# The first unit's q projected from unsplit fp32 weights, the k and v weights split first, and small loads moved back

## What is computed

```python
x = x + layernorm(attn(layernorm(x), w_qkv, b_qkv, w_out, b_out))
x = x + layernorm(ffn(layernorm(x), gate_w, up_w, down_w, scales))
# attn: 16 heads of 32, chunks of 128 tokens
qkv = x @ w_qkv.T + b_qkv                        # 3 x 512 outputs
out = (q * decay_q) @ S + ((q @ k.T) * dmask) @ v    # per chunk
S   = lam_c * S + (k * decay_k).T @ v
# ffn: silu(x @ gate * gs) * (x @ up * us) @ down * ds
```

## Time and profile before

| | |
|---|---|
| time of the runs | 993.68 us median of 3 (993.26 to 994.0) |
| profiled execution: its time | 993.01 us |
| profiled execution: its span | 991.2 us |
| PE busy | 957.7 us (97%) |
| DVE busy | 694.2 us (70%) |
| POOL busy | 686.9 us (69%) |
| ACT busy | 507.8 us (51%) |

### The profile page before, as it was taken

How to read it: one execution, slowest core, us unless ns; L and a number is a source line. 1 busy time by engine, 2 the same in 40 slices (tenths; PEclk the granted TensorE clock), 3 DMA queues, 4 the chain that set the end, 5 groups by cost and what they waited for, 6 DMA issues and landing times.

```text
span 991.2 us, 21995 instructions
## 1 busy us (share of the span) xinstructions
PE 957.7 (97%) x8498; PEld 709.6 (72%) x8498; DVE 694.2 (70%) x1355; ACT 507.8 (51%) x985; POOL 686.9 (69%) x837
## 2 busy tenths in 40 slices
PE   7999999999887999999999999999999999999996
PEld 6777778776665776777677677767767776776764
DVE  6999998875878766767676676767667676765422
ACT  3656665565555544646354464635446463544522
POOL 2689999887666765859476585947658594765733
PEclk9999999999998999999999999999999999999999
DMA  9899899999598784837558383866838486612200
GB/s 314 214 274 271 257 276 294 283 255 289 150 203 202 151 163 92 192 72 175 120 131 165 87 192 79 167 124 132 182 66 191 85 166 125 128 55 43 39 28 22
DMA packets 297641, 159.88 MB, mean 161 GB/s; under 512 B 141632, under 2 KB 272832, under 8 KB 297408
## 3 DMA queue, kind: packets, MB, share of 16 engines
q1 hardware_dynamic: 296672, 157.86, 67.5%
q10 hardware_dynamic: 864, 0.61, 0.2%
HBM read 82.93 MB, written 41.94 MB: 126 GB/s over the span
## 4 chain that ended last, share of the span: by engine, by line
PE 58%; DVE 17%; issue 10%; POOL 9%; ACT 4%; DMA 1%; POOLq 0%; SPq 0%; DVEq 0%; ACTq 0%
PE bank L845 17%; PE bank L827 12%; PE bank L720 9%; PE bank L735 8%; PE att L720 7%; POOL att_pool L996 4%; DVE stats L1249 3%; DVE p L1290 3%; DVE state_hl L1320 3%; DVE w_pool L1380 2%; ACT w_pool L562 2%; POOL rstd L937 2%; POOL w_pool L1010 2%; PE att L804 2%; DVE state L1309 1%
## 5 line engine op out<-in xcount | busy, mean ns | idle before, releaser
L827 PE MATMUL bank<-f_pool,gate_q 128*128 128x256 f16 x1536 | 183.9, 273 | 4.5 <-ACT w_pool L562 4.1
L827 PE MATMUL bank<-f_pool,up_q 128*128 128x256 f16 x1536 | 183.5, 273 | 1.4
L845 PE MATMUL bank<-down_q,w_pool 128*128 128x512 f16 x768 | 168.3, 379 | 0.0
L827 PEld LDWEIGHTS bank<-f_pool,gate_q 128*128 128x128 f16 x1536 | 146.9, 98 | 26.8 <-ACT w_pool L562 6.7
L827 PEld LDWEIGHTS bank<-f_pool,up_q 128*128 128x128 f16 x1536 | 149.3, 98 | 22.1 <-DVE w_pool L1380 5.0
L996 POOL TENSOR_TENSOR att_pool<-p,att_pool 128x512 f16<-128x512 f32 x128 | 145.7, 1160 | 26.3 <-ACT att_pool L516 26.3
L1380 DVE SCALAR_TENSOR_TENSOR w_pool<-bank,us_t,w_pool 128x256 f32<-128x256 f32 x192 | 84.1, 480 | 112.5 <-PE bank L827 54.1
L934 POOL TENSOR_TENSOR rstd<-mv,eps_t 128x1 f32<-128x1 f32 (+1 forms) x112 | 30.0, 268 | 182.6 <-DVE mv L1252 182.6
L845 PEld LDWEIGHTS bank<-down_q,w_pool 128*128 128x128 f16 x768 | 74.0, 98 | 87.0
L1010 POOL TENSOR_TENSOR w_pool<-w_pool 128x512 f16<-128x512 f32 x96 | 111.3, 1163 | 28.8 <-ACT w_pool L568 28.8
L516 ACT CAST att_pool<-p 128x512 f16<-128x512 f32 x128 | 75.5, 615 | 56.4 <-DVE p L1290 56.4
(11 more groups left out here) (143 smaller groups left out, 1824.9 us busy)
## 6 DMA issues: line engine op xcount, KB each, us to landing
xr<-in_x SPq DMA_DIRECT2D x32, 512.0 KB, 4.6
dram_qk<-qk_hl SPq DMA_DIRECT2D x64, 256.0 KB, 3.4
att_pool<-dram_qk SPq DMA_DIRECT2D x64, 256.0 KB, 5.6
f_pool<-dram_qk SPq DMA_DIRECT2D x64, 256.0 KB, 5.6
dram_kd<-kd_hl SPq DMA_DIRECT2D x32, 256.0 KB, 3.0
dram_v<-vv SPq DMA_DIRECT2D x32, 256.0 KB, 3.5
qn_pool<-dram_qk SPq DMA_DIRECT2D x32, 256.0 KB, 6.3
out_x<-w_pool SPq DMA_DIRECT2D x32, 256.0 KB, 2.1
```

Of the source, the lines that this page charges most:

```text
L827: ins = nc.tensor.matmul(b[:, j * TOK:(j + 1) * TOK], w[:, k, o * P:(o + 1) * P], x1_hl[:, v % 2, part, k], start=(k == 0 and part == 0), ...
L845: ins = nc.tensor.matmul((b_gate, b_up)[t][:, :], h_hl[:, part, k, t * P:(t + 1) * P], down_q[:, k], start=(k == 0 and part == 0), stop=(k ...
```

## The change

For unit 0 the four q outputs are no longer three 16-bit products each but one fp32 product: PE transposes the normalised x of unit 0 itself (`turn_first`), ACT copies it out of the bank into `x_first`, and `project_first` multiplies it with the weights as they were loaded, unscaled. ACT applies the scale while it reads the result (`scale=small[:, 11:12]`). The 136 constant products become 58. The weight split goes k, v, q instead of q, k, v, and ACT normalises x of unit 1 between k and v. The biases of v and the three scales are loaded by ACT later; the bias maximum is read from a table of 12 columns. x of unit 0 is loaded and normalised tile by tile. The product that spreads the maximum of the output weights moves from unit 2 to unit 3.

```diff
+            def turn_first(t):
+                pe.wait_ge(nrm_d[LN_X], t + 1)
+                for k in range(KT):
+                    ins = nc.tensor.transpose(b_s[t][:, k * P:(k + 1) * P], x_src(0)[:, t, k * P:(k + 1) * P], eye)
+                ins.then_inc(x_first_mm, 1)
+
+            def project_first(o):
+                for k in range(KT):
+                    ins = nc.tensor.matmul(qk_bank(0, o // 2)[:, o % 2 * TOK:(o % 2 + 1) * TOK],
+                                           w_stage[:, k, o * P:(o + 1) * P], x_first[:, k], start=(k == 0),
+                                           stop=(k == KT - 1))
+                if o % 2:
+                    ins.then_inc(qk_mm, 1)
...
-                if i == 0:
+                if i == 0 or n == 0 and i == 2:
                     pe.wait_ge(*x_landed(n))
+                if n == 1 and i == 0:
+                    pe.wait_ge(w_lo_d, 6)
...
-                        if n == 0 and j == 0 and (i == 0 and k % 2 == 0 or i == 2 and k == 0):
-                            pe.wait_ge(w_lo_d, i + k // 2 + 1 if i == 0 else 4)
+                        if n == 0 and i == 2 and j == 0 and k % 2 == 0:
+                            pe.wait_ge(w_lo_d, k // 2 + 1)
...
-                    pe.wait_ge(w_lo_d, 6)
+                    pe.wait_ge(w_lo_d, 4)
...
-                if k == 2:
+                if k == 3:
                     spread_wout_max()
-                project_qk(k, 0)
-                project_qk(k, 1)
+                if k:
+                    project_qk(k, 0)
+                    project_qk(k, 1)
...
-            for n in range(100):
-                nc.tensor.matmul(b_up[:, 0:2 * P], warm[:, 0:P], warm, start=True, stop=True)
+            constant_products(40)
+            pe.wait_ge(eye_in, 16)
+            turn_first(0)
+            constant_products(6)
+            turn_first(1)
+            constant_products(12)
+            pe.wait_ge(x_first_d, 2)
+            for k in range(KT):
+                pe.wait_ge(w_in[k], 16)
+            project_first(0)
             spread_w_max()
-            for n in range(36):
-                nc.tensor.matmul(b_up[:, 0:2 * P], warm[:, 0:P], warm, start=True, stop=True)
+            project_first(1)
+            project_first(2)
+            project_first(3)
...
-            act.dma_start(bv[:, :], b_v).then_inc(bias_in, 16)
+            act.wait_ge(eps_d, 3)
+            nc.scalar.activation(small[:, 63:64], eps_t[:, 0, 0:1], ACT.Silu)
+            x_normalise_tile(0, 0)
+            x_hi_tile(0, 0)
+            x_normalise_tile(0, 1)
+            x_first_tile(0)
+            x_hi_tile(0, 1)
+            x_first_tile(1)
+            act.dma_start(bv[:, :], b_v).then_inc(bv_in, 16)
...
-            x_normalise(0)
-            x_hi(0)
             act.wait_ge(w_scale_d, 1)
-            for part in range(3):
+            for part in (1, 2, 0):
                 for half in range(2):
                     w_hi(third(wqkv_hi, part, half), third(w_stage, part, half))
-            x_normalise(1)
-            x_hi(1)
+                if part == 1:
+                    x_normalise(1)
+                    x_hi(1)
...
+                dve.wait_ge(bias_in, 16)
+                link(nc.vector.tensor_reduce(col(7), bqk[:, :], AX.X, ALU.max, apply_absolute_value=True))
+                nc.vector.tensor_scalar(col(4), col(7), 1.0 / 256.0, None, ALU.mult)
...
-                    if k == 1:
-                        dve.wait_ge(bias_in, 16 * N_BIAS)
-                        nc.vector.tensor_reduce(col(7), bqk[:, :], AX.X, ALU.max, apply_absolute_value=True)
-                        link(nc.vector.tensor_reduce(col(8), bv[:, :], AX.X, ALU.max, apply_absolute_value=True))
-                        link(nc.vector.tensor_tensor(col(7), col(7), col(8), ALU.max))
-                        nc.vector.tensor_scalar(col(4), col(7), 1.0 / 256.0, None, ALU.mult)
...
-                link(nc.vector.tensor_scalar(bv[:, :], bv[:, :], col(11), None, ALU.mult))
-                for part in range(3):
-                    for half in range(2):
-                        w_lo(2 * part + half, third(wqkv_lo, part, half), third(wqkv_hi, part, half),
-                             third(w_stage, part, half))
...
-            moments_x(0)
+            for t, landed in enumerate((x_first_in, x_in[0])):
+                dve.wait_ge(landed, 16)
+                moments(LN_X, t + 1, x_src(0)[:, t], t)
```

More of the change, by code:

```diff
@@ L72, in sandwich @@
         lam = sb("lam", [P, KT])
[L73 removed]
+        bqk = sb("bqk", [P, 3 * KT])
         bv = sb("bv", [P, D])
@@ L407, in ahead @@
                         sp.dma_start(dst, src).then_inc(tab_in, 16)
-            load_x(0)
+            for t, landed in enumerate((x_first_in, x_in[0])):
+                sp.dma_start(x_src(0)[:, t], x_u[0, :, t]).then_inc(landed, 16)
             for k in range(KT):
@@ L461, in normalised, with x_normalise_tile, x_hi_tile, x_first_tile @@
                                             bias=rstd[:, ln, 1, t:t + 1])
+            def x_normalise_tile(n, t):
+                act.wait_ge(rs_d[LN_X], n + 2 if n else t + 1)
+                normalised(LN_X, x_src(n)[:, t], x_src(n)[:, t], t).then_inc(nrm_d[LN_X], 1)
             def x_normalise(n):
-                act.wait_ge(rs_d[LN_X], n + 1)
                 for t in range(T):
-                    normalised(LN_X, x_src(n)[:, t], x_src(n)[:, t], t).then_inc(nrm_d[LN_X], 1)
+                    x_normalise_tile(n, t)
+            def x_hi_tile(n, t):
+                act.wait_ge(nrm_d[LN_X], 2 * n + t + 1)
+                nc.scalar.copy(x_half(n)[:, t, 0], x_src(n)[:, t]).then_inc(x_hi_d, 1)
+            def x_first_tile(t):
+                act.wait_ge(x_first_mm, t + 1)
+                nc.scalar.copy(x_first[:, :, t * P:(t + 1) * P],
+                               b_s[t].rearrange("p (k c) -> p k c", k=KT)).then_inc(x_first_d, 1)
             def x_hi(n):
@@ L477, in q_hi @@
                 at_least(act, q_lo_d, 2 * (n - 1) + i + 1)
+                if n == 0:
+                    act.wait_ge(w_lo_d, 1)
                 for j in range(2):
@@ L480, in q_hi @@
                     ins = nc.scalar.activation(q32[:, i, j], qk_bank(n, i)[:, j * TOK:(j + 1) * TOK],
-                                               ACT.Identity, bias=bqk[:, o:o + 1])
+                                               ACT.Identity, bias=bqk[:, o:o + 1],
+                                               scale=1.0 if n else small[:, 11:12])
                 ins.then_inc(q_d, 1)
@@ L700, in spread_wout_max, with constant_products @@
                 ins.then_inc(wout_max_all, 1)
+            def constant_products(count):
+                for n in range(count):
+                    nc.tensor.matmul(b_up[:, 0:2 * P], warm[:, 0:P], warm, start=True, stop=True)
+            def turn_first(t):
[10 more added lines that the diff above has]
+                    ins.then_inc(qk_mm, 1)
             def project_qk(n, i):
-                if i == 0:
+                if i == 0 or n == 0 and i == 2:
                     pe.wait_ge(*x_landed(n))
+                if n == 1 and i == 0:
+                    pe.wait_ge(w_lo_d, 6)
                 if n < LEAD:
@@ L947, in inverse_std_x, with inverse_std_first @@
                 at_least(pool, nrm_d[LN_X], 2 * n)
-                inverse_std(LN_X, n + 1, slice(0, T))
+                inverse_std(LN_X, n + 2, slice(0, T))
+            def inverse_std_first(t):
+                pool.wait_ge(mv_d[LN_X], t + 1)
+                inverse_std(LN_X, t + 1, slice(t, t + 1))
             def inverse_std_of(ln, u, t):
@@ L1022, in _ @@
             pool.wait_ge(eps_d, 3)
-            inverse_std_x(0)
+            for t in range(T):
+                inverse_std_first(t)
             x_lo(0)
@@ L1156, in prepare_qkv @@
                 dve.wait_ge(w_scale_d, 1)
-                nc.vector.tensor_scalar(bqk[:, :], bqk[:, :], col(11), None, ALU.mult)
+                link(nc.vector.tensor_scalar(bqk[:, :], bqk[:, :], col(11), None, ALU.mult))
+                for n, part in enumerate((1, 2, 0)):
+                    for half in range(2):
+                        w_lo(2 * n + half, third(wqkv_lo, part, half), third(wqkv_hi, part, half),
+                             third(w_stage, part, half))
+                dve.wait_ge(bv_in, 16)
                 link(nc.vector.tensor_scalar(bv[:, :], bv[:, :], col(11), None, ALU.mult))
-                for part in range(3):
-                    for half in range(2):
-                        w_lo(2 * part + half, third(wqkv_lo, part, half), third(wqkv_hi, part, half),
-                             third(w_stage, part, half))
                 link(nc.vector.tensor_tensor(col(12), col(10), col(10), ALU.mult))
@@ L1174, in magic @@
                 at_least(dve, f_q_d, n - 1)
+                if n == 0:
+                    dve.wait_ge(qk_mm, 2)
                 buf = f_magic[n % 2]
@@ L1548 @@
         "w_qkv_t": np.asarray(L0_attn_w_qkv).T,
```

(2 more changed lines are left out.)

17 lines of the change are left out of this document (10 added, 7 removed).

## The result

| | before | after |
|---|---|---|
| median of 4 runs | 993.47 us (993.03 to 994.0) | 999.88 us (998.93 to 1001.21) |
| profiled execution: span | 991.2 us | 999.4 us |
| PE busy | 957.7 us | 959.4 us |
| DVE busy | 694.2 us | 693.0 us |

The changed kernel takes 1.006 times as long, 95% interval [1.0045, 1.0074]. That is outside the predicted range, on the other side of zero.

The account below looks back on a forecast made before the run. The lead was taken as PE alone, almost without waits; of 8.0 us offered, 5.7 would be taken (3.93 bank margin plus DVE's 1.8), so 993.68 - 5.7 = 988.0 us, range 985.4 to 991.2.

Parts of the forecast that it names:

- PE's side: Start of the lead: fp32 products end at 19.9 us, scale near 17.1, k of unit 0 ends 8.0 us earlier.
- The term of the loads: At the start: issuing two 256 KB loads later lets the last weight quarter land 1.3 us sooner, near 12.5.
- DVE's side: First units: DVE reaches unit 2's moments at 28.7 us, 1.8 us earlier; two column operations take 0.2 us each.
- What is left: After the start: PE catches the other engines, waits for banks, and keeps 3.93 + 1.8 = 5.7 us.
- the ring: DVE, ACT, POOL and SP in the first units, late by their own work; claimed to move 1.8 us earlier.
- The bank waits: PE waits of about 1 us each for `k_lo` in units 1 and 2, 2 to 2.5 us together.
- the subtraction at unit 11: Second transpose lands at 192.5 us, q starts at 195.87: 3.4 us margin, plus 2.3 is 5.7 again.
- the gain is carried to the end: Behind the lead all waits are between engines, so the 5.7 us gained stays to the end.
- (b): Rival: late loads or unit 11's transposes leave a smaller gain, 989.3 to 991.9 us, middle 990.8; chance 0.22.
- (a): Rival: the other engines give more than granted and PE takes all 8.0 us, 985.7 us; chance 0.12.
- (d): Rival: low halves end later, DVE's gain is negative and a bank wait eats the rest, 993.5 us; chance 0.07.
- (c): Rival: TensorE's clock at half rate for the fp32 products and k of unit 0, 996.3 us; chance 0.07.

Follow-up runs that it names:

- the fastest kernel: The changed kernel, later tiles realigned by an unused tile, SP turning unit 1's x before two feed-forward pieces and the output weights: 987.96 us.
- the good order: SP's start order of the fastest kernel: unit 1's x turned before two feed-forward pieces and the output weights; 987.96 us with aligned tiles.
- the last kernel: The changed kernel as given, tiles still 32 bytes off, with SP's start order from the fastest kernel: 1000.11 us.
- the realigned kernel: The changed kernel plus an unused tile behind the bias table that puts later tiles back on multiples of 256 bytes: 992.42 us.

## Why the prediction was wrong

- **PE's side** was right: the scale and k of unit 0 to 0.1 us, the end of the fp32 products to 0.3. The term of the loads was too small: the last quarter would have landed at 14.76 with them early, 2.5 us later and not 1.3; that 12.5 came out right (12.45) was luck, since it was reached from a 13.8 where the trace before has 14.04 and that kernel 14.76.
- **DVE's side** was right: 28.96 against 28.7, and the two column operations at 0.16 us.
- **What is left** named the right mechanism (the ring moves, PE catches it and waits for the bank of k) and the right size where nothing else stands in the way: 5.4 us in the lead and 5.8 in the median of the fastest kernel, for 5.7 forecast. The bank waits came to 1.4 us, where I had said 2 to 2.5, and a wider margin at the bank (the kernel with the output weights later) gained nothing, so the margin was not the only limit.
- **The step that failed** is the one that took the transfers as unchanged: the subtraction at unit 11 used the landing times of before, and "the gain is carried to the end" rests on them. Its second term, the 2.3 us by which the ring was to have moved at unit 11, was read from no row: it is what makes 3.4 up to 5.7. In the changed kernel the same bytes move at 247 instead of 271 GB/s, since a table grew by 16 bytes and pushed the tiles of the spills and reloads off their multiples of 256 bytes. PE then waits 2.19 and 0.68 us for the turned x of units 10 and 11, and 4.78 us for ACT at 256 us. Alone the moved tiles cost 7.5 us on the kernel before; on top of the good order they cost 12.1 (1000.11 - 987.96), because they also take the start's gain.
- **A second miss** was in the lead's first units. I checked when DVE and the ring let PE go on, but not when the turned x of units 0 and 1 lands for a PE 8 us ahead. That transfer stands behind the pieces and the output weights. Putting it ahead of them goes with 4.5 us on aligned tiles (992.42 to 987.96).
- **The rivals.** (b) came with the sign that it was given, waits of PE for turned x in units 10 and 11 (and in unit 1, which I had not named), but its price of 989.3 to 991.9 supposed transfers delayed by the start's loads and a full queue, not slower ones (its middle is 990.6, not the 990.8 given; nothing hangs on it); with aligned tiles the given order ends at 992.42, just above it. (a) and (d) did not come. (c), the half rate, did not come at the fp32 products but after PE's waits: 1.7 us too much in unit 10 (7.08 for 5.40), 2.2 at 256 us (4.99 for 2.78), and 2.9 at the first output projection (8.21 for 5.35). The last two, 5.1 us, lie in the 8.1 that this execution lost between 244 and 294 us. In the last kernel, with a granted clock of 0.93 against 0.86 between 250 and 300 us, the profiled execution took 999.26 us against 1001.21. The granted clock of every execution says the same: its mean is 0.9875 in the four of the changed kernel and 0.992 in those of before. By an estimate from these means, taking PE as always busy, the lower clock costs 4.8 of the 6.4 us. The half rate stands behind the waits, and with the tiles moved alone it comes too (0.86 between 250 and 300 us), so it is a part of what they cost and not a rival to them. No run took it away while the tiles stayed moved.
- **Left open:** why a 512-byte packet takes 8 ns more at 32 bytes and 3 at 128; why the two sides moved alone cost 5.0 us and both together 7.5; and what the waits would cost without the clock that falls after them (the same estimate gives the clock 5.5 of the 12.1 us).

## What to carry to other kernels

When a diff changes the size of any tile, compare the addresses of all later tiles before and after; an unused tile that brings them back to multiples of 256 bytes is a one-line test, and here it is worth 7.5 us. An engine that is given a head start meets every wait it never met: for each thing that it needs in the next two units, the transfers too, read when that arrives. And a gain at the start is kept only if the stage that follows isn't bound by something else, so compare GB/s per stage, not only bytes. Slower transfers cost time only where an engine waits for them: here that is the lead and what stands right behind it, not the 600 us after.

## What the runs showed that I had not expected

- 512-byte packets into SBUF rows that start 32 bytes beyond a multiple of 256: 47 ns median against 39. Out of SBUF: a mean of 28 to 30 against 27. In this kernel both together are 0.76% of the time, 7.5 of 993.66 us.
- TensorE's granted clock fell to its half rate (1.2 of 2.4 GHz; stretches with 0.52 to 0.63) after waits of 2.12 us (33.80 in the realigned kernel), 2.19 (177.85 in the changed one), 4.27 (14.89) and 4.78 (256.07), but not after one of 1.85 us (177.62 in the last kernel). Before, 3.1 us of idle time at 14.27 did not lower it, nor did 3.40 us ahead of the first output projection (5.35 us for its 24 products), where the changed kernel waited 3.43 us and took 8.21. So the length of the last wait alone does not decide it.
- Two kernels with the same code up to a point need not land their transfers alike. The second transpose of x of unit 0 landed at 18.3 to 18.8 us in three of the kernels and at 21.0 to 21.3 in three others. In the first three SP issued it 0.10 to 0.14 us behind ACT's last load of the scales, in the others 0.16 to 0.36 us ahead of it, and nothing in the program orders the two. That the order is the cause is not shown.
